# Layer-norm steps, z projections and GpSimd products moved to other slots of a fused Mamba and mixture-of-experts kernel

## The reference, cut to what matters

```python
mod = (_silu(c) @ wmod).reshape(16, 6, 1, -1)
sa, ca, ga, sb, cb, gb = (mod[:, k] for k in range(6))
h  = _layernorm(x) * (1 + ca) + sa
xn = _layernorm(h) * norm_g + norm_b            # inside the Mamba block
# for xn and for xn reversed in time, each with its own weights (256 inner channels, 16 states):
u, z = split(xn @ Win.T);  u = silu(conv4(u) + convb)
dtr, B, C = split(u @ Wx.T);  dt = softplus(dtr @ Wdt.T + bdt);  A = -exp(Alog)
s[t] = exp(dt[t] * A) * s[t-1] + (dt[t] * u[t]) * B[t];  y[t] = sum_n s[t] * C[t]
out = ((y + u * D) * silu(z)) @ Wout.T
x = x + ga * (h + out_forward + out_backward)
h2 = _layernorm(x) * (1 + cb) + sb
x = x + gb * (weighted sum of the 2 best of 8 experts(h2) + shared expert(h2))
```

## Time and profile before

| what | value |
|---|---|
| time, median of 3 runs | 2438.02 us (2435.1 to 2441.28) |
| time of the profiled execution | 2438.78 us |
| its span, first to last instruction | 2437.0 us |
| VectorE busy | 2220.6 us (91%) |
| TensorE busy, weight loads | 2079.6 us (85%), 1332.5 us (55%) |
| GpSimd busy | 2023.3 us (83%) |
| ScalarE busy | 1522.8 us (62%) |
| mean granted TensorE clock | 0.919 of full speed |

### The profile page before, as it was taken

The page is one execution under the profiler, slowest core; times in us unless marked ns, Lnnn a source line. Parts: engine busy times, 40 slices in busy tenths (PEclk is TensorE's granted clock), DMA queues, the critical chain, the costliest instruction groups (busy, mean ns, idle before and its releaser), DMA issues. The chain is left out here.

```text
span 2437.0 us, 32077 instructions
## 1 busy us (share of the span) xinstructions
PE 2079.6 (85%) x10085; PEld 1332.5 (55%) x10085; DVE 2220.6 (91%) x3530; ACT 1522.8 (62%) x2499; POOL 2023.3 (83%) x1334
## 2 busy tenths in 40 slices
PE   6678988889898888989888898888989888898868
PEld 2445655655565555655555565555656555565555
DVE  4999999999999999999999999999999999999952
ACT  4557666576666666666676666667665666666533
POOL 2768889888898898889889898988989899887845
PEclk7689989999898999989999998999989999998989
DMA  5333444433344433434343344343344333443410
GB/s 149 133 138 124 136 135 135 143 118 134 129 134 136 136 125 129 141 128 142 128 136 123 130 143 136 125 139 128 128 129 142 136 122 129 135 136 124 139 49 27
DMA packets 124061, 312.43 MB, mean 128 GB/s; under 512 B 19700, under 2 KB 46308, under 8 KB 123892
## 3 DMA queue, kind: packets, MB, share of 16 engines
q1 hardware_dynamic: 123892, 310.39, 38.1%
HBM read 303.74 MB, written 6.60 MB: 127 GB/s over the span
## 5 line engine op out<-in xcount | busy, mean ns | idle before, releaser
L495 POOL TENSOR_TENSOR bt<-v,bb 128x1024 f32<-128x1024 f32 x511 | 1205.2, 2360 | 104.3 <-DVE psA L941 89.7
L941 DVE TENSOR_TENSOR_SCAN psA<-psA,bt 128x512 f32<-128x512 f32 x1024 | 1195.8, 1213 | 83.1 <-ACT psA L680 65.3
L680 ACT ACTIVATE psA<-dt,aneg 128x512 f32<-128x512 f32 x1024 | 688.0, 688 | 591.8 <-DVE g L951 589.6
L1199 PEld LDWEIGHTS psY<-ident,g 128*128 128x128 f32 x4096 | 506.9, 150 | 495.2 <-DVE g L951 301.2
L1199 PE MATMUL psY<-ident,g 128*128 128x128 f32 x4096 | 602.2, 291 | 190.3 <-DVE g L951 189.2
L951 DVE TENSOR_TENSOR g<-psA,cb 128x512 f32<-128x512 f32 x1024 | 671.6, 675 | 0.0
L585 POOL TENSOR_TENSOR act<-pf,gf 128x512 f32<-128x512 f32 x288 | 366.1, 1271 | 171.7 <-DVE pf L1044 143.6
L1311 PE MATMUL F<-h2T,w 128*128 128x512 f32 x576 | 334.5, 664 | 91.7 <-DVE pf L1044 91.5
L1361 PE MATMUL F<-w,act 128*128 128x128 f32 x2304 | 308.5, 277 | 10.6 <-POOL act L585 10.5
L1361 PEld LDWEIGHTS F<-w,act 128*128 128x128 f32 x2304 | 281.9, 192 | 24.0 <-POOL act L585 18.2
L1215 PE MATMUL psP<-xnT,wcT 128*128 128x512 f32 x496 | 257.7, 645 | 0.1
(11 more groups left out here) (186 smaller groups left out, 1978.4 us busy)
## 6 DMA issues: line engine op xcount, KB each, us to landing
bb<-bc_rows SPq DMA_DIRECT2D x256, 512.0 KB, 3.7
cb<-bc_rows SPq DMA_DIRECT2D x256, 512.0 KB, 3.6
wB<-w_rows SPq DMA_DIRECT2D x80, 256.0 KB, 4.1
x<-in_L_attn_x SPq DMA_DIRECT2D x16, 256.0 KB, 4.4
out_x<-osb SPq DMA_DIRECT2D x16, 256.0 KB, 4.6
modA<-mod_table SPq DMA_DIRECT2D x15, 192.0 KB, 4.7
w<-in_L_ffn_ew SPq DMA_DIRECT2D x2, 1024.0 KB, 7.3
bc_rows<-xd SPq DMA_DIRECT2D x32, 64.0 KB, 3.3
```

The lines of the kernel that those rows point to most:

```text
L495: g.tensor_tensor(bt[:, n % 2, :, :], v[d][:, :, :], bb[:, n // 2 % 2, n % 2, :].unsqueeze(1).broadcast_to([P, NH, T]), ALU.mult).then_inc ...
L680: s.activation(psA[:, half * T:half * T + T], dt_[d][:, half, :], ACT.Exp, scale=aneg[d][:, half, n:n + 1]).then_inc(a_s, 1)
L941: w.tensor_tensor_scan(ah, ah, bt[:, n % 2, half, :][:, order], 0.0, ALU.mult, ALU.add)\
L1199: last = m.matmul(psY[:, half * T + i * P:half * T + i * P + P], g_[:, n % 2, half, i * P:i * P + P], ident[:, :], is_transpose=True, star ...
```

## The change

Only slots and the order of some instructions change; the arithmetic and the number of instructions stay.

| piece | engine | slot before | slot after |
|---|---|---|---|
| statistics of x / of the first norm's result | VectorE | 3 / 8 | 2 / 5 |
| moments of the two norms | GpSimd | 4 / 9 | 3 / 6 |
| first norm, scale and shift | ScalarE, GpSimd | 6, 7 | 3, 4 |
| last step of the second norm | ScalarE | 10 | 11 |
| z of direction 0: projection and tanh | TensorE, ScalarE | 29, 30 | 30, 30 |
| z of direction 0: last step | VectorE | 30, 31 | 31, 31 |
| hx, two products | GpSimd | 23, 31 | 31, 31 |
| wg / output of batch b-2 | GpSimd | 6 / 0 | 7 / 1 |
| loads of modF and modC, store of the output | SyncE | 0 | 2 |

```diff
-Z_SLOTS, ZS_SLOTS = ((29, 30), (2, 5)), ((30, 31), (6, 6))
-STAT_SLOT, RSTD_SLOT, Z1_SLOT, H1_SLOT, STAT2_SLOT, RSTD2_SLOT, XNORM_SLOT, XN_SLOT = 3, 4, 6, 7, 8, 9, 10, 12
-HX_SLOTS, WG_SLOT = (23, 31), 6
+Z_SLOTS, ZS_SLOTS = ((30, 30), (2, 5)), ((31, 31), (6, 6))
+STAT_SLOT, RSTD_SLOT, Z1_SLOT, H1_SLOT, STAT2_SLOT, RSTD2_SLOT, XNORM_SLOT, XN_SLOT = 2, 3, 3, 4, 5, 6, 11, 12
+HX_SLOT, WG_SLOT = 31, 7
+OUT_SLOT, MODF_SLOT = 1, 2
...
                     if slot == 0:
-                        early(b, scan, ffn, last)
+                        if scan and not last:
+                            load(b + 1)
+                    if ffn and slot == MODF_SLOT:
+                        ffn_rows(b - 1)
...
-                    if slot == 0 and not (isinstance(b, int) and b < 2):
+                    if slot == MODF_SLOT and b >= 2:
                         store(b - 2)
...
-            def early(b, scan, ffn, last):
-                if ffn:
-                    fb = b - 1
-                    wait(sp, o_s, 2 * fb)
-                    row = mod_dram[bass.ds(fb, 1), 5 * D:6 * D].broadcast_to([P, D])
-                    sp.dma_start(modF[:, :], row).then_inc(modF_in, 16)
...
-                if scan and not last:
-                    load(b + 1)
+            def ffn_rows(fb):
+                wait(sp, o_s, 2 * fb)
+                row = mod_dram[bass.ds(fb, 1), 5 * D:6 * D].broadcast_to([P, D])
+                sp.dma_start(modF[:, :], row).then_inc(modF_in, 16)
...
-                    if slot == 0 and not (isinstance(b, int) and b < 2):
+                    if slot == OUT_SLOT and b >= 2:
                         output(b - 2)
```

More of the change, by code:

```diff
@@ L447, in scales @@
                     scale_row(fb, e + 2)
-            def early(b, scan, ffn, last):
-                if ffn:
-                    fb = b - 1
-                    wait(sp, o_s, 2 * fb)
-                    row = mod_dram[bass.ds(fb, 1), 5 * D:6 * D].broadcast_to([P, D])
-                    sp.dma_start(modF[:, :], row).then_inc(modF_in, 16)
-                    with nc.allow_non_contiguous_dma(reason="two columns"):
-                        sp.dma_start(modC[:, :], mod_dram[bass.ds(fb, 1), 3 * D:5 * D]
-                                     .rearrange("a (k p) -> p (a k)", p=P)).then_inc(modF_in, 16)
-                if scan and not last:
-                    load(b + 1)
+            def ffn_rows(fb):
+                wait(sp, o_s, 2 * fb)
+                row = mod_dram[bass.ds(fb, 1), 5 * D:6 * D].broadcast_to([P, D])
+                sp.dma_start(modF[:, :], row).then_inc(modF_in, 16)
+                with nc.allow_non_contiguous_dma(reason="two columns"):
+                    sp.dma_start(modC[:, :], mod_dram[bass.ds(fb, 1), 3 * D:5 * D]
+                                 .rearrange("a (k p) -> p (a k)", p=P)).then_inc(modF_in, 16)
             def store(fb):
@@ L523, in norms @@
                     g.tensor_tensor(z1[:, :, :], xn[:, :, :], over_tiles(modA[:, 0, :]), ALU.add).then_inc(h1_s, 1)
-                if slot == HX_SLOTS[0]:
+                if slot == HX_SLOT:
                     wait(pool, hxK_s, b)
                     g.tensor_tensor(hx[:, :, :], z1[:, :, :], over_tiles(modA[:, 2, :]), ALU.mult).then_inc(hx_s, 1)
-                if slot == HX_SLOTS[1]:
                     pool.wait_ge(hx_s, 2 * b + 1)
@@ L621, in _ @@
             pool.wait_ge(ga_in, 16)
-            norms(0, HX_SLOTS[0])
-            norms(0, HX_SLOTS[1])
+            norms(0, HX_SLOT)
             pool.wait_ge(bt_s, 1)
@@ L701, in turn_z @@
             def turn_z(b, d, slot):
[L703 to L706, removed]
+                for half in range(NH):
+                    if slot == Z_SLOTS[d][half]:
+                        act_e.wait_ge(z_full, 4 * b + 2 * d + half + 1)
+                        s.activation(th[:, 2 + half, :], (F0, F1)[half][:, :], ACT.Tanh).then_inc(zt_s, 1)
             def prep(b, d, k):
@@ L1230, in project_z @@
             def project_z(b, d, slot):
[L1232 to L1239, removed]
+                for half in range(NH):
+                    if slot == Z_SLOTS[d][half]:
+                        if d == 0:
+                            wait(pe, (pf_s, F1_free)[half], 2 * NE * (b - 1))
+                        else:
+                            pe.wait_ge(z_free, 4 * b + half + 1)
+                        m.matmul((F0, F1)[half][:, :], wzT[d][:, half, :], xnT[:, PAD:PAD + T], start=True, stop=True)\
+                            .then_inc(z_full, 1)
             def skip_and_turn(bank, d, half):
```

## The result

The changed kernel takes 2497.66 us (median of 4 runs, 2496.32 to 2499.78) against 2436.56 us; the ratio is 1.0249, with a 95% interval of 1.0231 to 1.0267. It is 61 us slower. The profiled execution took 2496.32 us with a span of 2494.5, 57.5 more than before.

What follows compares the result with a forecast made beforehand. VectorE, busy 2220.6 of 2437.0 us, was taken as the bound, so only waits could change. Terms 11.8 + 1.65 + 15.9 + 8.0 = 37.4 us on 2438.78 gave 2476, rounded to 2475; range 2452 to 2500, chance 0.72.

Steps and rivals of the forecast that it cites:

- TensorE's clock: Gap before the projection, 2.2 us, lowers the granted clock in one body of four: 8.0 us, ends 0 and 32.
- Nothing waits behind the logarithm that the change moves: Slots 11 and 30: VectorE waits for tables and logarithm, not xn; waits of about 1.7 us stay unchanged.
- Rival 3: Waits behind the logarithm, slots 11 and 30, go: 2390 us, or 2419 with the first two terms paid; chance 0.05.
- The wait for x: Slot 2: statistics of x wait 0.84 us a batch for the load, 11.8 us for 14; batch 0 adds 1.65.
- Rival 1: x lands in time for slot 2's statistics, so nothing waits for the load: 2455 us; chance 0.09.
- The cover of the chain to x2: Slots 2 to 4: statistics ahead of gate_y leave VectorE waiting for x2; net 1.14 us a batch, 15.9 for 14.
- today's share: The wait for x2 already in the kernel before, 2.4 us or 0.17 a batch, subtracted from the predicted 1.31.
- rival 2: Before the projection, TensorE's granted clock falls in every body, costing 32 us: 2500 us; chance 0.08.
- The zero terms: Norms in slots 3 to 6, xn in slot 11, moved z and GpSimd's moved work: each taken as 0 us.
- the moved z: Slot 31: VectorE's two pieces of z there instead of one in 30 and one in 31, same work: 0.
- hx in slot 31: GpSimd's next bt ends some 1.3 us later but just fits before slot 1's scan: 0, or up to 0.2 a batch.
- xn in slot 11: VectorE's product about 0.2 us late, set against a short bt wait in slot 14: 0, ends -0.2 and +0.3.

Runs made afterwards that it cites:

- the run with the norms back: Changed kernel with the six steps of the two norms put back to slots 3, 4, 6, 7, 8 and 9, other moves kept: 2439.84 us, ratio 1.0012.
- the run with the load first: Changed kernel with SyncE issuing the loads of x and modA at the head of slot 0, before the load of cb: 2462.36 us, ratio 1.0105.

## Why the prediction was right, and where it was off

The direction, the places and the range (2452 to 2500) were right; the point, 2475, was 23 us low. The time lies only 2.3 us inside the range, and that it lies inside is partly luck: the range's upper end gave TensorE's clock 32 us, and the clock took 17.5; the rest of the way was made by terms that I had too small or at 0. By my terms a body should have been 2.55 us longer (0.84 + 1.14 + 0.57); it was 4.28. In its own steps:

- *Nothing waits behind the logarithm that the change moves.* Right. The wait in front of slot 11 stayed 1.69 us in the changed kernel and with xn moved alone. Rival 3 is out.
- *The wait for x.* Right in kind, in 15 bodies, but sized too small: 19.6 - 2.2 = 17.4 us against 13.2 (11.8 + 1.42). The mean was 1.12 us a body, not 0.84. I had taken the median landing, 4.4 us, where a sum of waits goes by the mean, 4.5 before and 4.7 after; two late landings, of 6.2 and 5.8, cost 2.55 and 2.14 us. Rival 1, the load in time, is what issuing it first brought about, not the change itself. The prediction set the Trainium skill's 2.6 us against this term; since that section is about DMAs issued by GpSimd, it never bore on a load that SyncE issues.
- *The cover of the chain to x2.* Right: 0.88 + 0.23 us a body against 1.08 + 0.23, before today's share goes off. The last body's row was a good measure. What I left out is the overlap lost at the new waits, 0.16 us a body in slots 2 and 3.
- *TensorE's clock.* The mechanism was right, its size not: I counted one body in four at 2.3 us, 8 us in all; it was 11 in 14 at 1.6, 17 to 18 us. I had taken the gap as 2.2 us. In the body shown it was 3.10: the wait for x is 1.25 instead of 0.84; gate_y ends at 624.52 in the trace before, not at the 624.4 that I used; from gate_y's end (643.81) to the first product it is another 0.10, which I had left out; and the sums in front end 0.3 us earlier against VectorE's products than before. How often the clock falls could not be read from the trace before. The result lies next to rival 2, which I gave 0.08, but not by rival 2's road.
- *The zero terms.* Two were right: the moved z cost nothing, and hx in slot 31 costs 0.05 us in slot 0. With the statistics gone from slot 8, the first pf of slot 9 waits for its tanh, 0.20 us a body, within the ends that I gave. xn in slot 11 was the wrong zero. Its pf is 0.24 us later, as I had said, but I had set against that the short wait in front of slot 14's scan, 0.22, which did not end: one of 0.53 for the exponentials took its place. Together 0.54 us a body, 7.6 us, above the upper end of 0.3. In the run with the norms back, the same two slots cost 0.40.

The terms as measured, for 14 bodies: 15.7 for the load, 3.2 and 2.2 for slot 3 and the lost overlap, 10 for the cover, 17.5 for the clock, 2.8 for slot 9, 7.6 for xn and 0.7 for hx, together 59.7 of the 59.9. Batch 0 adds 3.2, and the start and the tail take 5.6 off in this execution, which is the 57.5 us between the two spans; the medians lie 61 us apart.

## What to carry to other kernels

A wait at which an engine stands says when its work is late, not what is in its way: look at whether anything stands between the slow step and the waiting one before moving work out of that slot. Before a piece is moved forward, look at what it is the cover for where it stands, and at what is written behind it in the new slot; behind the gate product instead of in front of it the same statistics cost 46 us less. Where the wait itself can't be shortened, moving work into it pays, but count what the moved work's followers push aside on the next engine.

## What the runs showed of the hardware

- TensorE's clock turned on gaps that differ little, and not on their length alone. In front of the same eight products it never fell behind gaps of 1.72 to 1.76 us (14 bodies of the run with the load first); in the changed kernel it fell behind gaps of 2.27, 2.44, 2.52, 2.67, 2.69 and all of 2.96 or more, and stayed up behind 2.61, 2.65 and 2.73. What else decides in between, no run shows. Where it fell, the first eight products took up to 2.05 us instead of 1.13, the second eight up to 1.92 instead of 1.06. Products whose result nobody reads, put into the gap, made the kernel 17 us faster, from 2497.7 to 2481.0.
- The same load of x landed in 2.5 to 3.3 us in the 14 bodies in which it was issued 2.5 us or more behind the load before it, and in 4.1 to 6.2 where it was issued 0.36 us behind a load of 512 KB.
- On VectorE an instruction that waits for nothing starts before the one in front of it has ended (623.25 against 623.32). Behind a wait that is lost, 0.16 us a body in slots 2 and 3 of the changed kernel, and busy time grew by 5.3 us with the same instructions.
